# Ternary weights by a cap and a floor in 8-bit numbers instead of three passes, and a new order of the work, in a fused cross-attention and feed-forward kernel

## The reference

```python
def weight_quant(w):
    scale = 1.0 / jnp.clip(jnp.mean(jnp.abs(w)), 1e-05)
    q = jnp.clip(jnp.round(w * scale), -1.0, 1.0) / scale
    return w + jax.lax.stop_gradient(q - w)
...
x = x + jnp.tanh(g_xattn[0]) * _L0_xattn_ref(_layernorm(x, axis=-1), ctx_768, mask_BxS2_bk0, L0_xattn_W_q, ...)
x = x + jnp.tanh(g_ffn[0]) * _L0_ffn_ref(_layernorm(x, axis=-1), L0_ffn_w1, L0_ffn_b1, L0_ffn_w2, L0_ffn_b2)
```

## Time and profile before

| | us |
|---|---|
| median of 3 runs | 1194.61 |
| lowest, highest | 1194.42, 1195.01 |
| profiled execution, whole time | 1197.4 |
| profiled execution, span of its instructions | 1195.6 |
| mean granted clock of PE | 0.974 of full speed |

### The profile page before, as it was taken

One profiled execution on the slowest core, in us unless ns is written; L12 is line 12 of the kernel. 1 busy time (PEld: TensorE's weight loads), 2 busy tenths in 40 slices (PEclk: granted clock), 3 DMA queues, 4 the chain that ended last, 5 costly groups with the idle time before them and its releaser, 6 DMA issues.

```text
span 1195.6 us, 25997 instructions
## 1 busy us (share of the span) xinstructions
PE 1108.5 (93%) x9060; PEld 682.8 (57%) x9060; DVE 989.6 (83%) x1877; ACT 942.5 (79%) x1527; POOL 803.8 (67%) x739
## 2 busy tenths in 40 slices
PE   5798979999999989999999998999999998999687
PEld 3455655666555655565565665566665665665343
DVE  6799878989888787988889888888989878787954
ACT  6987666978969767796978969697987967798655
POOL 3789757576775766767585777758676676757820
...
GB/s 330 211 261 263 245 184 218 182 272 196 217 199 210 245 188 249 205 210 225 190 265 159 250 266 202 219 211 230 181 262 201 209 258 210 201 172 251 266 109 27
DMA packets 116753, 258.47 MB, mean 216 GB/s; under 512 B 13072, under 2 KB 80400, under 8 KB 116240
## 3 DMA queue, kind: packets, MB, share of 16 engines
...
...
## 4 chain that ended last, share of the span: by engine, by line
PE 49%; DMA 21%; issue 8%; ACT 7%; DVE 7%; POOL 6%; SPq 3%; DVEq 0%; ACTq 0%; POOLq 0%
PE ps_g L559 23%; DMA pt<-away 13%; PE ps_g L612 8%; DMA away<-blocks 7%; PE ps_g L647 5%; PE ps_g L656 5%; PE ps_s L589 4%; DVE blocks L801 3%; SPq L529 3%; POOL p L1058 3%; ACT prob L920 2%; ACT p L929 1%; PE ps_g L679 1%; DVE st L776 1%; POOL p L1053 1%
## 5 line engine op out<-in xcount | busy, mean ns | idle before, releaser
L1058 POOL TENSOR_TENSOR p<-prob,p 112x750 f16<-112x750 f32 x256 | 425.0, 1663 | 146.2 <-ACT p L929 137.5
L801 DVE STREAM_TRANSPOSE blocks<-p 128x768 f32<-128x768 f32 x256 | 246.8, 969 | 20.7 <-POOL p L1058 18.7
L739 DVE CUSTOM_DVE_ANT_0 prob<-ps_s,mbias 112x750 f32<-112x750 f32 x256 | 230.8, 926 | 16.8 <-PE ps_s L589 13.8
L920 ACT ACTIVATE prob<-prob,rmin 112x750 f32<-112x750 f32 x256 | 233.0, 912 | 4.6 <-DVE rmin L739 4.3
L559 PE MATMUL ps_g<-ctx,wk 128*128 128x375 f16 x1152 | 207.3, 326 | 6.0 <-POOL ctx L1069 5.0
L559 PE MATMUL ps_g<-wv,ctx 128*128 128x512 f16 (+1 forms) x864 | 203.5, 381 | 1.6 <-DVE q_sb L768 1.2
L612 PE MATMUL ps_g<-pt,v_sb 128*64 128x256 f16 x2304 | 149.7, 284 | 34.2 <-DMA pt<-away 33.9
L929 ACT ACTIVATE p<-prob 112x750 f16<-112x750 f32 x160 | 167.2, 1045 | 13.3 <-DVE blocks L801 12.8
L589 PE MATMUL ps_s<-k_sb,q_sb 64*112 64x375 f16 x1536 | 152.7, 332 | 12.5 <-DVE rmin L739 12.4
L559 PEld LDWEIGHTS ps_g<-ctx,wk 128*128 128x128 f16 x1152 | 111.6, 98 | 92.0 <-issue 12.2
L612 PEld LDWEIGHTS ps_g<-pt,v_sb 128*64 128x64 f16 x2304 | 134.6, 113 | 40.8 <-issue 40.1
...
## 6 DMA issues: line engine op xcount, KB each, us to landing
away<-blocks SPq DMA_DIRECT2D x512, 192.0 KB, 3.3
pt<-away SPq DMA_DIRECT2D x128, 768.0 KB, 6.2
...
```

Source lines behind the costliest of these rows:

```text
L739: nc.vector.tensor_tensor_reduce(prob[:, (b * NU + n) % PROBS, :].rearrange("p (c k) -> p c k", c=2), ps_s[0:HT, n % 2, :, 0:CH], mbias[:, ...
L801: nc.vector.transpose(b_words[:, step % MOVED, :, :, n % 2, :].rearrange("p g t q -> p t g q"), p_words[:, (b * NU + n) % HILO, :].rearran ...
L920: nc.scalar.activation(prob[:, (b * NU + n) % PROBS, :], prob[:, (b * NU + n) % PROBS, :], ACT.Exp, bias=rmin[:, n:n + 1], scale=-1.0, acc ...
L1058: nc.gpsimd.tensor_tensor(p16[0:HT, u % HILO, 0:J, 1], prob[:, (b * NU + n) % PROBS, :], p16[0:HT, u % HILO, 0:J, 0], ALU.subtract).then_i ...
```

## The change

It does two things.

First, the ternary weights take two passes. `WB` on POOL now multiplies by the reciprocal times 2^-9 and takes the smaller of that and 2^-9. `WQ` on DVE takes the larger of that and -2^-9 and writes fp8; 2^-9 is the smallest number that this fp8 has, so the conversion itself rounds to -2^-9, 0 or 2^-9. `WR` on ACT is gone, with `above` and the constant `one_up`. `WQ` now reads the fp32 piece and not a bf16 one. `WM` gets one more instruction of one column on DVE, which multiplies the reciprocal, and the scales `sm2` and `smh` take 2^-9 back with no instruction more. What waited for `w_above` waits for `w_quant`. The first piece of `w1` is loaded into `hq` and no longer into its own place.

Second, `SLOTS`, `START`, `END` and some stages hold another order. `LX` is now three batches ahead, `XL` and the first `XT` two.

```diff
-MAGIC = 12582912.0
+TERN = 2.0 ** -9
...
-    [("S", 5), ("PV", 0), ("N1", 0), ("TR", 7), ("L3", 1), ("GM", 0), ("T", 5), ("GS", 0), ("K", 3), ("V", 2),
+    [("V", 1), ("U", 3), ("VL", 0), ("VL", 1), ("XB", 0), ("L4", 1), ("T", 4), ("E", 9), ("F1", 0), ("TR", 7),
...
-        W1_AT = [own[0], own[1], halves_of_b1[0], halves_of_b1[1], halves_of_h[0], halves_of_h[1], halves_of_xr[0],
+        W1_AT = [hq[:, :].bitcast(F32), w1[:, 4 * WCH:8 * WCH].bitcast(F32), halves_of_b1[0], halves_of_b1[1], halves_of_h[0], halves_of_h[1], halves_of_xr[0],
...
-                        sp.wait_ge(w_above, COMES_AFTER[n] + 1)
+                        sp.wait_ge(w_quant, COMES_AFTER[n] + 1)
...
-                    nc.vector.reciprocal(winv[:, at:at + 1], wmean[:, at:at + 1]).then_inc(w_inv, 1)
+                    nc.vector.reciprocal(winv[:, at:at + 1], wmean[:, at:at + 1]).then_inc(w_rec, 1)
+                    dve.wait_ge(w_rec, n + 1)
+                    nc.vector.tensor_scalar(winv[:, at:at + 1], winv[:, at:at + 1], TERN, None, ALU.mult)\
+                        .then_inc(w_inv, 1)
...
                 if kind == "WQ":
-                    dve.wait_ge(w_above, n + 1)
-                    nc.vector.tensor_scalar(piece((w2, w1)[n // NW], n), above[n % 2], 2.0, -1.0, ALU.min, ALU.add,
+                    dve.wait_ge(w_near, n + 1)
+                    nc.vector.tensor_scalar(piece((w2, w1)[n // NW], n), FLOATS[n], -TERN, None, ALU.max,
                                             saturate=False).then_inc(w_quant, 1)
...
-                if kind == "WR":
-
-                    act.wait_ge(w_near, n + 1)
-                    if n >= 2:
-                        act.wait_ge(w_quant, n - 1)
-                    nc.scalar.activation(above[n % 2], FLOATS[n], ACT.Relu, bias=one_up[:, :]).then_inc(w_above, 1)
-                    return
...
-                    nc.gpsimd.tensor_scalar(FLOATS[n], FLOATS[n], winv[:, at:at + 1], MAGIC, ALU.mult, ALU.add)\
+                    nc.gpsimd.tensor_scalar(FLOATS[n], FLOATS[n], winv[:, at:at + 1], TERN, ALU.mult, ALU.min)\
                         .then_inc(w_near, 1)
```

More of the change, by code:

```diff
@@ L160 @@
[L160 to L163, removed]
+    N1:0:0 XN:0:0 LX:0:0 LC:0:0 PD:0:0 CX:0:0 PW:0:0 LC:1:0 CX:1:0 XT:0:0 CX:2:0 XT:1:0 LC:2:0 XL:0:0 XL:1:0 MB:0:0
@@ new lines @@
+    PW:1:0 PD:1:0 KL:0:0 KL:1:0 L:0:0 QL:0:0 M:0:0 PW:2:0 PD:2:0 L:1:0 K:0:0 M:1:0 K:1:0 Q:0:0 PW:3:0 K:2:0 PD:3:0
+    WA:0:0 E:0:0 M:2:0 S:0:0 M:3:0 LM:0:0 TR:0:0 K:3:0 E:1:0 WL:0:0 QL:1:0 S:1:0 H:0:0 H:1:0 WL:3:0 KL:2:0 WA:1:0
+    Q:1:0 KL:3:0 WG:0:0 TR:1:0 WA:2:0 V:0:0 H:2:0 LM:0:1 WL:1:0 S:2:0 WA:3:0 WL:2:0 E:2:0 M:4:0 M:5:0 BD:0:0 L:2:0
+    N1:0:1 WA:4:0 WL:5:0 LX:0:1 WA:5:0 E:3:0 WL:4:0 WA:6:0 H:3:0 WA:7:0 WL:6:0 L:3:0 WL:7:0 V:1:0 Q:2:0 TR:2:0
+    WB:0:0 WB:1:0 VL:0:0 L:4:0 E:4:0 WB:2:0 V:2:0 XN:0:1 WB:3:0 WL:11:0 WL:8:0 WM:0:0 QL:2:0 E:5:0 H:4:0 TR:3:0
@@ new lines @@
+    S:3:0 Q:3:0 R:0:0 VL:1:0 H:5:0 WQ:0:0 LC:0:1 WQ:1:0 VL:2:0 WA:8:0 K:4:0 E:6:0 WB:4:0 QL:3:0 K:5:0 L:5:0 WB:5:0
+    WB:6:0 M:6:0 TR:4:0 H:6:0 KL:4:0 V:3:0 XT:0:1 WQ:2:0 M:7:0 WA:9:0 K:6:0 WA:10:0 KL:5:0 XT:1:1 H:7:0 XL:0:1
+    S:4:0 VL:3:0 K:7:0 E:7:0 M:8:0 E:8:0 TR:5:0 WA:11:0 WL:9:0 V:4:0 KL:6:0 LC:1:1 WQ:3:0 CX:0:1 WL:10:0 L:6:0
+    WA:12:0 KL:7:0 XL:1:1 T:0:0 L:7:0 CX:1:1 WQ:4:0 WQ:5:0 V:5:0 Q:0:1 WQ:6:0 WA:13:0 VL:4:0 M:9:0 E:9:0 TR:6:0
+    WB:7:0 CX:2:1 VL:5:0 WL:13:0 M:10:0 QL:0:1 TR:7:0 T:1:0 L:8:0 H:8:0 WB:8:0 WA:14:0 WL:12:0 M:11:0 L:9:0 WA:15:0
@@ new lines @@
+    S:5:0 T:2:0 H:9:0 E:10:0 WL:15:0 Q:1:1 WB:9:0 S:6:0 WM:1:0 K:0:1 PV:0:0 E:11:0 R:1:0 E:12:0 QL:1:1 KL:0:1
+    H:10:0 H:11:0 TR:8:0 L:10:0 E:13:0 WL:14:0 WB:10:0 K:1:1 LC:2:1 U:0:0 L:11:0 M:12:0 V:0:1 PA:0:0 K:2:1 TR:9:0
+    H:12:0 WQ:7:0 N1:0:2 M:13:0 V:1:1 S:7:0 U:1:0 LC:0:2 TR:10:0 WB:11:0 KL:1:1 WQ:8:0 V:2:1 VL:0:1 KL:2:1 U:2:0
+    TR:11:0 L:12:0 T:3:0 E:14:0 VL:1:1 M:14:0 H:13:0 PL:0:0 K:3:1 L:13:0 V:3:1 WB:12:0 WQ:9:0 S:0:1 M:15:0 E:15:0
+    H:14:0 KL:3:1 LX:0:2 T:4:0 R:2:0 U:3:0 TR:12:0 VL:2:1 U:4:0 MB:0:1 T:5:0 U:5:0 PV:1:0 TR:13:0 L:14:0 T:6:0
@@ new lines @@
+    WQ:10:0 M:0:1 H:15:0 VL:3:1 WQ:11:0 M:1:1 U:6:0 KL:4:1 K:4:1 E:0:1 PA:1:0 QL:2:1 M:2:1 KL:5:1 K:5:1 Q:2:1
+    TR:14:0 M:3:1 WB:13:0 WB:14:0 L:15:0 WB:15:0 S:1:1 H:0:1 TR:15:0 V:4:1 E:1:1 VL:4:1 XN:0:2 K:6:1 E:2:1 L:0:1
+    WQ:12:0 WQ:13:0 H:1:1 CX:0:2 WQ:14:0 T:7:0 U:7:0 K:7:1 TR:0:1 LR:1:0 L:1:1 V:5:1 H:2:1 KL:6:1 VL:5:1 KL:7:1
+    TR:1:1 R:3:0 LC:1:2 LX:0:3 LR:0:1 PL:1:0 PV:2:0 M:4:1 Q:3:1 M:5:1 S:2:1 E:3:1 PA:2:0 H:3:1 WQ:15:0 TR:2:1
+    LC:2:2 XL:0:2 TR:3:1 T:0:1 L:2:1 XT:0:2 PL:2:0 E:4:1 L:3:1 H:4:1 XB:1:0 QL:3:1 XL:1:2 BD:1:0
@@ L181 @@
+    HT:0:-2 GE:1:-2 XB:1:-1 PV:3:-1 PL:3:-1 PA:3:-1 U:6:-1 GM:1:-2 GS:1:-2 G2:1:-2 HT:1:-2 G3:1:-2 O:0:-1 U:7:-1
+    L2:0:-1 O:1:-1 L3:0:-1 L2:1:-1 L4:0:-1 F2:0:-2 XQ:0:-1 L3:1:-1 HT:2:-2 L4:1:-1 F1:0:-1 F1:1:-1 F1:2:-1 XQ:1:-1
+    F1:3:-1 GE:0:-1 GS:0:-1 F1:4:-1 F1:5:-1 HT:3:-2 F1:6:-1 GE:1:-1 F1:7:-1 GM:0:-1 G2:0:-1 G3:0:-1 GS:1:-1 GM:1:-1
+    F2:1:-2 HT:0:-1 HT:1:-1 G2:1:-1 G3:1:-1 F2:0:-1 HT:2:-1 HT:3:-1 F2:1:-1
 """, NB)
@@ L358, in build @@
         w_inv = sem("w_inv")
+        w_rec = sem("w_rec")
         w_near = sem("w_near")
-        w_above = sem("w_above")
         w_quant = sem("w_quant")
@@ L462, in build @@
         halves_of_b1 = [b1[:, n * WCH:(n + 1) * WCH] for n in range(2)]
-        own = [w1[:, n * 4 * WCH:(n + 1) * 4 * WCH].bitcast(F32) for n in range(2)]
         W2_AT = [halves_of_h[0], halves_of_h[1], halves_of_xr[0], halves_of_xr[1]] \
             + [pt_words[:, n * WCH:(n + 1) * WCH] for n in range(3)] + [v_words[:, KC * D:KC * D + WCH]]
-        W1_AT = [own[0], own[1], halves_of_b1[0], halves_of_b1[1], halves_of_h[0], halves_of_h[1], halves_of_xr[0],
+        W1_AT = [hq[:, :].bitcast(F32), w1[:, 4 * WCH:8 * WCH].bitcast(F32), halves_of_b1[0], halves_of_b1[1], halves_of_h[0], halves_of_h[1], halves_of_xr[0],
                  halves_of_xr[1]]
@@ L472, in build @@
         rough = [hqt[:, :, :].rearrange("p k q -> p (k q)").bitcast(BF16)[:, 0:WCH], xc[:, :].bitcast(BF16)]
-        above = [hq[:, :].bitcast(BF16)[:, n * WCH:(n + 1) * WCH] for n in range(2)]
         def piece(w, n):
@@ L494, in emit @@
                 elif kind == "BD":
-                    sp.wait_ge(w_above, NW + 4)
+                    sp.wait_ge(w_quant, NW + 4)
                     sp.dma_start(b1[:, :], b1_d[:].partition_broadcast(ROWS)).then_inc(d_b1, 16)
@@ L518, in emit @@
                     if t < HELD:
-                        sp.wait_ge(w_above, COMES_LAST[t // 2] + 1)
+                        sp.wait_ge(w_quant, COMES_LAST[t // 2] + 1)
                     need_dma(sp, d_out[t % HELD], t // HELD)
@@ L534, in emit @@
                     if step == 0:
-                        sp.wait_ge(w_above, NW - 1)
+                        sp.wait_ge(w_quant, NW - 1)
                     need_away(sp, step)
@@ L551, in _ @@
         def _(pe):
-            pe.wait_ge(consts, 7)
+            pe.wait_ge(consts, 6)
             def split_product(out, terms, tiles):
@@ L568, in emit @@
                     return
-                if kind in ("PD", "BD", "PW", "WA", "WB", "WG", "WL", "WQ", "WR"):
+                if kind in ("PD", "BD", "PW", "WA", "WB", "WG", "WL", "WQ"):
                     return
@@ L836, in emit @@
                     need_tile(dve, "x2_amp", t)
-                    nc.vector.tensor_scalar(sm2[:, c, 4:5], sm2[:, c, 3:4], 1.0 / (QMAX * UNIT), wmean[:, 0:1],
+                    nc.vector.tensor_scalar(sm2[:, c, 4:5], sm2[:, c, 3:4], 1.0 / (QMAX * UNIT * TERN), wmean[:, 0:1],
                                             ALU.mult, ALU.mult).then_inc(s["x2_scale"], 1)
@@ L868, in emit @@
                     need_tile(dve, "h_amp", t)
-                    nc.vector.tensor_scalar(smh[:, c, 4:5], smh[:, c, 3:4], 1.0 / (QMAX * UNIT), gw2[:, 0:1],
+                    nc.vector.tensor_scalar(smh[:, c, 4:5], smh[:, c, 3:4], 1.0 / (QMAX * UNIT * TERN), gw2[:, 0:1],
                                             ALU.mult, ALU.mult).then_inc(s["h_scale"], 1)
@@ L958, in emit @@
                         act.wait_ge(wready, 3)
-                        act.wait_ge(w_above, NW)
+                        act.wait_ge(w_quant, NW)
                     nc.scalar.activation(v_sb[0:KEYS[n], p, n, 0, :], g[0:KEYS[n], :], ACT.Copy, scale=VS / WS)\
@@ L1039, in emit @@
                     pool.wait_ge(w_inv, n // NW + 1)
-                    nc.gpsimd.tensor_scalar(FLOATS[n], FLOATS[n], winv[:, at:at + 1], MAGIC, ALU.mult, ALU.add)\
+                    nc.gpsimd.tensor_scalar(FLOATS[n], FLOATS[n], winv[:, at:at + 1], TERN, ALU.mult, ALU.min)\
                         .then_inc(w_near, 1)
                     return
-                if kind in ("PD", "BD", "PW", "WA", "WG", "WL", "WM", "WQ", "WR"):
+                if kind in ("PD", "BD", "PW", "WA", "WG", "WL", "WM", "WQ"):
                     return
```

46 lines of the change are left out of this document (12 added, 34 removed), and 63 rows, old and new, of tables (SLOTS, STAGE_OF_ITEM).

## The result

| | before | after |
|---|---|---|
| median, us | 1194.51 | 1243.83 |
| runs, lowest to highest | 4, 1185.76 to 1195.01 | 4, 1241.49 to 1250.15 |
| profiled execution, whole time | 1197.4 | 1241.49 |
| its span | 1195.6 | 1239.7 |
| mean granted clock | 0.974 | 0.966 |

The ratio is 1.0439, with a 95% interval of 1.0375 to 1.0503. The forecast was 1179 us and its range ended at 1191.

What follows compares the result with a forecast made beforehand. PE was taken to bound the middle, with start and tail a chain through all engines. Start -8, middle -9 and tail +1 made -16 us, from 1194.6 to 1179 us; range 1167 to 1191.

Steps and rivals of the forecast that it cites:

- the one on `WB`: Start, POOL's weight pass: multiplying and comparing costs the same as multiplying and adding at the same size, so nothing.
- The gain in the start: First 118 us: removing ACT's 18.4 us pass gives 8.5 us, less 0.5 for added DVE work, so 8 us.
- the 0.6 us charged to `WQ`: Start, DVE's weight pass: 0.6 us more for reading the wider fp32 source over 16 pieces.
- The price by the Trainium skill: Start, `WQ`: the skill's table halves the pace for fp32, costing 4.3 us for 16 pieces; the start would give 6 us.
- The second PV: Repeated batches: more cover ends PE's wait for `pt` there, 10 us gained plus 1.5 us of slowed clock.
- the rival of 1216 us: Middle: reload of `pt` behind the first `PV` binds at 9.0 us a load, making the kernel slower; chance 0.11.
- The fourth PV: Repeated batches: loses 2 us of cover from `TR` 15 and 0.5 from the third `PV`; charged 2.5 us.
- The tail: Last batch: cover sums the same within 0.5 us, but the second `PV` has 5.5 us for a 6.5 us load; 1 us lost.

Runs made afterwards that it cites:

- e1: The changed kernel with POOL's pass multiplying and adding instead of multiplying and taking the smaller, cap left out (weights not ternary): 1213.42 us, 1.0217 of before.
- e2: The changed kernel, whole computation, with cap and floor both on DVE and POOL only multiplying and adding zero: 1208.15 us, 1.0195 of before.
- e5: The kernel before with POOL's pass taking the smaller where it added (weights wrong): 1228.47 us, 1.0269 of before.
- e11: e2 with an ACT pass over 128x1024 16-bit values put back at the 16 places of `WQ`, its result unused: 1211.78 us, 1.0187 of before.
- e4: The order of before without `WR`, one `WQ` moved, with cap and floor on DVE and POOL only multiplying: 1220.37 us, no ratio.
- e9: e2 with the last K product (1.44 us) moved from ahead of the third `PV` to between third and fourth: 1192.1 us, 0.9990 of before.

## Why the prediction was wrong

**The step that failed first** is the one on `WB`: "multiplies and compares where it multiplied and added, at the same size: nothing". It was priced by size and not by a row with that operation, because the trace had none, and the text gave it neither a bound nor a rival. It measured 2.6 us more for each of 16 pieces. e1 and e2 give back 30.2 and 30.7 us of start, and in the old order e5 loses 32 us by its ratio. PE's idle time in the first 206 us, which was to fall by 8 us, rose from 36.5 to 54.2.

**The gain in the start**, 8 us, did not come even with that mended: e2's start is 119.7 against 120.1. ACT's busy time did fall by 15.2 us, and of the 0.6 us charged to `WQ` nothing is seen: its fastest takes 0.65 us, where 0.68 to 0.74 was said. e11 gives the pass some 7 us in one profile and nothing in the ratio, so that the term may be right for the pass; e4 did not get it from the old list, and e2 shows that the new list doesn't keep it.

**The price by the Trainium skill** (VectorE: DVE Perf Modes, "The perf-mode tier table"), 4.3 us more for the fp32 source, did not come: 128 x 1024 from fp32 to 8 bits takes 675 ns at its fastest and 687 in the median of the group shown, and from bf16 it took 677 at its fastest. The table has a column for bf16 and one for fp32 and none for a result of 8 bits; to price this form by its bf16 column was my step and not the page's.

**The second PV**, 11.5 us with its clock: right in its mechanism. The waits there are gone, and the reload behind the first `PV`, on which the rival of 1216 us rested, was no bound: the load of step 3 was issued 0.08 us behind the end of the first `PV`, took 4.8 us in the median of the 13 batches and landed 2.7 us ahead of the second `PV`, where 8.2 us is the load from which that rival decides. That rival had the sign and not the cause.

**The fourth PV**, charged at 2.5 us, is the term of the sum that was mis-sized. Two things were wrong in it. I had counted 15.7 and 13.7 us of cover from the place of `TR` 15 in the list. But DVE waits in order, and the item ahead waits for scores, so that in the instance above PE had 10.3 us left (558.79 to 569.05) for a chain of 13.0; in before it was 10.7 us in the median. The loss of cover was 0.4 us and not 2. And I had taken the chain to stay as it was, where it grew by 2.1 us, from 10.7 to 12.8, with the transfers that the new order puts beside the load. The 13 waits are 1.7 to 4.9 us long, and with them the sum doubled, from 20.8 to 42.8 us. With cover added in e9, it is worth 16 us by the medians and 24 by the ratios, each to the runs of before on its own chip. POOL's slow passes had no share in the middle that can be seen: after's is 994.8 us, and with the quick pass it is 986.3 to 996.4.

**The tail** was charged 1 us and gained 8.4; why was not tried.

The sum as the runs show it: POOL's operation from 1.0439 to 1.0195, some 29 us; cover at the fourth `PV` from 1.0195 to 0.999, some 24 us; and what was to be gained, in the start and at the second `PV`, taken up by the new list's own losses, of which the start's was not found.
